# An 8-head graph attention layer: target rows of four of a group's eight tiles gathered by GpSimd instead of spread by TensorE

## The chip, the cores and the metric

One core of a Trainium2 chip (trn2). The time is that of the device, in microseconds (us), for one execution of the whole program, seven graph layers one after the other; with several runs it is their median.

## The reference, cut to what matters

A graph of 3125 nodes with 256 features and 53125 edges (25000 pairs in both directions and a self loop for each node), the edges sorted by their target `dst`. Seven layers of message passing run one after the other: layer 0 is a graph attention layer with 8 heads and edge features, layers 1 to 3 are SAGE convolutions, layer 4 is a GCN, layers 5 and 6 are attention layers with 4 heads. The change touches layer 0 alone:

```python
h = (x @ W.T).reshape(n, H, D)                       # n = 3125, H = 8, D = 32
h_src, h_dst = h[src], h[dst]
alpha = einsum('ehd,hd->eh', h_src, a_src) + einsum('ehd,hd->eh', h_dst, a_dst)
enc = relu(edge_attr @ edge_W.T + edge_b).reshape(-1, H, D)
alpha = leaky_relu(alpha + sum(enc * h_dst, axis=-1), 0.2)
ex = exp(alpha - segment_max(alpha, dst)[dst])
attn = ex / segment_sum(ex, dst)[dst]
out = segment_sum(h_src * attn[..., None], dst) + bias
```

What the change is about is `h_dst`, the row of each edge's target node, which is multiplied by the encoded edge features `enc` and summed per head.

## The kernel before, in words

**Tiles and groups.** The edges are padded to 416 tiles of 128, and 8 tiles make a group, so that there are 52 groups in each layer. Since the edges are sorted by target, the targets of one tile lie within a window of 128 consecutive nodes, and those of a group are added to the accumulator `acc` window by window.

**The table.** Ahead of layer 0 the node rows are written to a table in HBM, `tables[0]`, with 272 floats a row: 8 scores, and for each of 8 heads one score and 32 features (together 264 floats, columns `H` to `TW`).

**Source rows.** POOL (GpSimd) gathers the rows of the source nodes with an indirect DMA for each tile (L1791), 8 a group, into one of four row buffers. From the fifth group on it waits first for `rows_free`, which VectorE gives in `add_group` (L1227) once a group has been added to the accumulator. POOL does this for all seven layers, and in layer 0 nothing else.

**Target rows.** For the target side, SyncE loads for each tile the 128 consecutive table rows of its window into `spans` (L1693, in `edge_tables`), two tiles a quarter, q = 0 to 3, each quarter with a semaphore `span_landed[q]` of its own. Ahead of a quarter's load it waits for `h_ready`, so that the quarter's spans of the group before have been read. VectorE makes one-hot matrices of the edges' targets (L1120), and TensorE spreads the window's rows to the edges with two matmuls a quarter (`spread`, L478; the profile shows each as two instructions). The result stands in PSUM, in `h_ps`, one buffer of two tiles, so a spread waits until VectorE has used the quarter before (`prod_ready`).

**Encoding, product and sum.** TensorE also encodes the edge features (`encode`, L465), ScalarE takes them out of PSUM (`encoded`, L916), VectorE multiplies them by the target rows (`products`, L1128) and sums them per head (`reductions`, L1134).

**The order of a step.** Each engine has the order of a step written out by hand (`step`, in `edge_pe`, `edge_act` and `edge_dve`), for three groups at once: group g is summed up, group n = g + 1 gets its scores and segment maxima, and group m = g + 2 gets its products. TensorE's step is: encode and spread quarter 0 of m, encode 1, the sums of g's first four tiles (L513), the transposed scores of n (L485), spread 1, encode 2, the edges of the scans (L490), spread 2, encode 3, the carries (L497), the sums of g's other four tiles, spread 3, the shifts turned back (L502), the sums turned (L526, L527) and the rescaling (L507). VectorE's step is: messages of g (L1182), the one-hots of g + 3, `add_group` of g - 1 (L1196, L1198), product 0, scores of n, messages, reduction 0, scans (L1149, L1150), product 1, carry (L1156 to L1162), reduction 1, product 2, maxima (L1167 to L1173), reduction 2, rescale, product 3 and reduction 3. ScalarE takes the node sums out of PSUM at L933, as soon as `node_ready` says that L513 is done.

Of the kernel before, what the change touches and what calls it, by code (L numbers as in the profile page):

```python
# [28 lines left out]
ALU = mybir.AluOpType  # L29
# [18 lines left out]
TW = D + 16  # L48
# [20 lines left out]
ATTR = 4 * PAD_E // P  # L69
HEAD = D // 8 + 1  # L70
ASIDE = 16 * (4 + 3 * 4)
SUM_BUFS = 4
# [12 lines left out]
def gnn_program(nc, a, out, stop):  # L85
    last_stage = NL - 1 if stop is None else stop
    ctx = ExitStack()
    with ctx:
# [139 lines left out]
        src_landed = [sem(f"src_landed{b}") for b in range(SUM_BUFS)]  # L228
        span_landed = [sem(f"span_landed{q}") for q in range(4)]
        high_landed = [sem("high_landed0"), sem("high_landed1")]  # L230
# [217 lines left out]
        def edge_pe(pe, l, turns, sum_turns):  # L448
# [19 lines left out]
            def spread(m, j, h, q):  # L468

                par, turn = pair_of(j, h)  # L470
                if q == 0:
                    pe.wait_ge(edge_turned_ready, m + 1)
                pe.wait_ge(span_landed[q], 32 * (m + 1))
                if not (q == 0 and isinstance(m, int) and m == 0):
                    pe.wait_ge(prod_ready, 4 * m + q)
                for i in range(2):
                    k = 2 * q + i
                    ins = mm(ps[:, i, 0:TW], edge_turned[:, par, k, :], spans[:, k, :], start=True, stop=True)  # L478
                ins.then_inc(h_ready, 1)
# [628 lines left out]
        def edge_dve(dve, l, ch, turns, sum_turns):  # L1108
# [14 lines left out]
            def products(m, q):  # L1123

                at = 4 * m + q
                dve.wait_ge(enc_copied, at + 1)
                dve.wait_ge(h_ready, at + 1)
                V.tensor_tensor(prod[:, q % 2, :, :], enc[:, q % 2, :, :], h_ps[:, :, H:TW], ALU.mult).then_inc(prod_ready, 1)  # L1128

# [501 lines left out]
        def _(sp):  # L1631
# [45 lines left out]
            def edge_tables(x, h, par):  # L1677
# [9 lines left out]
                sp.dma_start(attr[:, par, :], attr_parts[:, bass.ds(x * T * P, T * P)]).then_inc(attr_landed[par], 16)  # L1687
                for q in range(4):
                    if not (early and x == 0):
                        sp.wait_ge(h_ready, 4 * x + q - 3)  # L1690
                    for k in (2 * q, 2 * q + 1):
# [39 lines left out]
        def _(pool):  # L1731
# [41 lines left out]
            for l in range(n_edge_layers):  # L1773
# [10 lines left out]
                for g in range(NG):  # L1784
# [5 lines left out]
                    for k in range(T):  # L1790
                        pool.indirect_dma_start(  # L1791
                            src_rows(l, par)[:, k, :], None, tables[l][:, :],
                            bass.IndirectOffsetOnAxis(ap=src_idx[:, g * T + k:g * T + k + 1], axis=0)
                            ).then_inc(src_landed[par], 16)


# [178 lines left out]
```

## Time and profile before

| what | value |
|---|---|
| time, median of 3 runs | 6083.94 us (6080.36 to 6095.35) |
| profiled execution, its own time | 6029.88 us |
| its span, first to last instruction | 6028.1 us |
| granted TensorE clock, mean over the span | 0.721 of full speed |
| busy share of the span, PE, DVE, ACT, POOL | 57%, 35%, 19%, 47% |
| HBM read, written | 512.47 MB, 31.37 MB |

A page of the profile shows one execution. Engines: PE is TensorE's matmuls, PEld its weight loads, DVE is VectorE, ACT ScalarE, POOL GpSimd, SP SyncE. L1791 is line 1791 of the kernel. A row of a group of instructions gives engine, operation, what it writes and reads, count, busy time and mean length of one in ns, then the idle time of its engine just ahead of it and what ended that. "remote" stands where the profile finds no instruction whose end released the wait at that moment. Layer 0 lies between some 83 and 1070 us of the span.

### The profile page before, as it was taken

Reading aid. Unit: us, or ns where it says so; the run is one execution under the profiler, and the core shown is the slowest. Engines: PE = TensorE matmul, PEld = TensorE weight load, DVE = VectorE, ACT = ScalarE, POOL = GpSimd, SP = SyncE. Lnnn points to the kernel's source line nnn. Section 1 sums busy time; section 2 is a strip of 40 time slices with the busy share of each in tenths; the row PEclk is TensorE's granted clock in tenths of the full one; section 3 lists DMA queues with packets and bytes.
Section 4 is the critical chain, followed back from the end, with each engine's and each line's share of the span. In section 5 each row is a group of like instructions: output and inputs, shape, how many; then the busy total and the mean of one; then the engine's idle time right before and its main releaser. Section 6 shows DMA issues by size and latency. Waiting matters only on the chain.

```text
span 6028.1 us, 63366 instructions
## 1 busy us (share of the span) xinstructions
PE 3460.3 (57%) x14514; PEld 2370.1 (39%) x14515; DVE 2116.7 (35%) x5850; ACT 1164.2 (19%) x3033; POOL 2826.4 (47%) x3013
## 2 busy tenths in 40 slices
PE   4777778835446444454446644444665663665665
PEld 2555455524334333333334433333443442443443
DVE  3666666512111111111113211123444444444445
ACT  1333333200001000010000100003332323332232
POOL 2444444066553665646663366643554532444540
PEclk7878888767668766777667777776666776766676
DMA  5555555022222222223222223222333322333330
GB/s 172 146 143 145 140 142 146 19 87 87 79 80 74 86 86 84 86 80 86 84 84 59 67 84 87 86 58 76 91 92 91 93 72 66 90 91 92 93 84 22
DMA packets 278630, 546.82 MB, mean 91 GB/s; under 512 B 72195, under 2 KB 161079, under 8 KB 278111
## 3 DMA queue, kind: packets, MB, share of 16 engines
q0 software_dynamic: 140416, 391.24, 23.4%
q1 hardware_dynamic: 137951, 152.85, 8.6%
q8 instruction: 71, 1.16, 0.1%
q14 instruction: 192, 1.57, 0.1%
HBM read 512.47 MB, written 31.37 MB: 90 GB/s over the span
## 4 chain that ended last, share of the span: by engine, by line
another core or an unknown queue 36%; PE 32%; issue 14%; DVE 10%; SPq 3%; ACT 2%; DVEq 1%; ACTq 1%; DMA 1%; POOL 0%; POOLq 0%
PE ps L606 9%; PE ps L690 7%; PE ps L857 3%; PE ps L513 2%; PE ps L835 2%; DVE rows L1409 2%; PE ps L478 2%; PE ps L805 1%; PE ps L613 1%; ACTq L338 1%; SPq L1692 1%; ACT rows L1026 1%; PE ps L816 1%; SPq L1693 1%
## 5 line engine op out<-in xcount | busy, mean ns | idle before, releaser
L1791 POOL DMA_INDIRECT rows<-table,src_idx x2912 | 2798.4, 961 | 2804.8 <-issue 864.7
L606 PE MATMUL ps<-rows,attr 128*128 128x256 f32 x3328 | 1068.6, 491 | 170.8 <-issue 100.1
L606 PEld LDWEIGHTS ps<-rows,attr 128*128 128x128 f32 x3328 | 825.7, 255 | 381.0 <-issue 208.7
L613 PE MATMUL ps<-ident,rows 128*128 128x128 f32 x416 | 116.7, 373 | 1184.6 <-ACT rows L1026 901.3
L1302 DVE TENSOR_TENSOR acc<-acc,ps 128x256 f32 x208 | 87.7, 422 | 1933.7 <-PE ps L613 1323.3
L613 PEld LDWEIGHTS ps<-ident,rows 128*128 128x128 f32 x416 | 51.0, 172 | 1267.9 <-ACT rows L1026 957.4
L1297 DVE TENSOR_SCALAR attr<-iota,local 128x128 f32<-128x128 f32 x1664 | 356.7, 298 | 219.2 <-issue 156.0
L690 PE MATMUL ps<-rows,attr 128*128 128x260 f32 x832 | 331.0, 551 | 33.7 <-DVE rows L1409 33.7
L690 PE MATMUL ps<-rows,w_roots 128*128 128x260 f32 x832 | 325.1, 544 | 35.5 <-DVE rows L1409 34.9
L478 PE MATMUL ps<-rT,attr 128*128 128x272 f32 x832 | 282.7, 470 | 63.0 <-DVE norm L1128 24.4
L1026 ACT ACTIVATE rows<-ps,mean_of 128x256 f32<-128x256 f32 x156 | 73.8, 473 | 1251.4 <-remote 824.6
L660 PE MATMUL ps<-ident,al 128*32 128x128 f32 x104 | 38.6, 371 | 467.1 <-DVE al L1372 457.6
L513 PE MATMUL ps<-rows,rT 128*128 128x272 f32 x832 | 296.5, 515 | 6.7 <-DVE rows L1182 6.6
L1371 DVE TENSOR_TENSOR al<-ps,rows 128x32 f32<-128x32 f32 x104 | 19.9, 191 | 679.3 <-remote 673.7
L1409 DVE TENSOR_TENSOR rows<-rows,ps 128x1024 f32<-128x1024 f32 x208 | 249.2, 1198 | 2.9 <-ACT rows L989 1.4
L690 PEld LDWEIGHTS ps<-rows,attr 128*128 128x128 f32 x832 | 211.8, 273 | 95.3 <-DVE rows L1409 38.7
L690 PEld LDWEIGHTS ps<-rows,w_roots 128*128 128x128 f32 x832 | 209.3, 270 | 95.7 <-DVE rows L1409 39.8
L513 PEld LDWEIGHTS ps<-rows,rT 128*128 128x128 f32 x832 | 197.2, 249 | 69.6 <-issue 15.6
L478 PEld LDWEIGHTS ps<-rT,attr 128*128 128x128 f32 x832 | 171.7, 224 | 130.7 <-issue 79.4
L1128 DVE TENSOR_TENSOR norm<-rT,ps 128x528 f32<-128x528 f32 x208 | 144.8, 696 | 191.4 <-PE ps L478 91.0
L660 PEld LDWEIGHTS ps<-ident,al 128*32 128x32 f32 x104 | 10.7, 103 | 497.5 <-issue 497.3
L977 ACT ACTIVATE w_roots<-iota,local 128x128 f32<-128x128 f32 x416 | 127.2, 388 | 390.5 <-DVEq L1452 390.5
(230 smaller groups left out, 4341.8 us busy)
## 6 DMA issues: line engine op xcount, KB each, us to landing
rT<-table SPq DMA_DIRECT2D x416, 136.0 KB
rows<-table,src_idx POOLq DMA_INDIRECT x2912
high_rows<-in_tiles SPq DMA_DIRECT2D x156, 256.0 KB
table<-rows SPq DMA_DIRECT2D x24, 512.0 KB, 2.8
table<-rows SPq DMA_DIRECT2D x12, 528.0 KB, 3.0
pens<-pen_rows SPq DMA_DIRECT2D x52, 96.2 KB
pens<-pen_rows SPq DMA_DIRECT2D x104, 48.1 KB
attr_parts<-acc SPq DMA_DIRECT2D x9, 416.0 KB
```

The lines of the kernel that those rows point to most:

```text
L478: ins = mm(ps[:, i, 0:TW], edge_turned[:, par, k, :], spans[:, k, :], start=True, stop=True)
L513: ins = mm(edge_node_ps[par], edge_hot[par][:, k, :], src_rows(l, b)[:, k, 0:TW], start=k == 0, stop=k == T - 1)
L606: ins = mm(node_ps[par % 2], sum_hot[:, par % 2, k, :], src_rows(l, par)[:, k, 0:D], start=k == 0, stop=k == T - 1)
L613: ins = nc.tensor.transpose(sum_ps[par % 2][f], node_sums[:, par % 2, f * P:(f + 1) * P], ident[:, :])
L690: ins = mm(gat_node_ps[par], gat_hot[par][:, k, :], src_rows(l, b)[:, k, 0:D + H], start=k == 0, stop=k == T - 1)
L857: ins = mm(into, x[:, f, k * P:(k + 1) * P], w_table[s + 1][:, f, 0:w], start=f == 0, stop=f == 1)
L977: ins = nc.scalar.activation(gat_hot[par][:, k, :], iota[:, 0:P], ACT.Abs, scale=-1.0, bias=local[:, bass.ds(g * T + k, 1)])
L1026: nc.scalar.activation(node_sums[:, par % 2, :], node_ps[par % 2], ACT.Copy, scale=mean_of[:, bass.ds(g, 1)] if l in MEAN_LAYERS else 1.0) ...
L1128: V.tensor_tensor(prod[:, q % 2, :, :], enc[:, q % 2, :, :], h_ps[:, :, H:TW], ALU.mult).then_inc(prod_ready, 1)
L1297: return V.tensor_scalar(sum_hot[:, par % 2, k, :], iota[:, 0:P] if w is None else iota[:, bass.ds(w * P, P)], local[:, bass.ds(g * T + k, ...
L1409: V.tensor_tensor(x[:, :, 0:D].rearrange("p t (h d) -> p t h d", h=H), x[:, :, 0:D].rearrange("p t (h d) -> p t h d", h=H), gat_ex_ps[b % ...
L1791: pool.indirect_dma_start(src_rows(l, par)[:, k, :], None, tables[l][:, :], bass.IndirectOffsetOnAxis(ap=src_idx[:, g * T + k:g * T + k + ...
```

## The change

In layer 0, the target rows of the quarters q = 2 and 3, tiles 4 to 7 of each group, are gathered by POOL with an indirect DMA for each tile, by `dst_idx`, straight into the `spans` buffer in SBUF: row e of the buffer is then the target row of edge e itself. TensorE's `spread` returns at once for these quarters, SyncE loads spans only for q = 0 and 1, and VectorE's `products` reads q = 2 and 3 from `spans` in place of PSUM. POOL issues these gathers behind the 8 source gathers of the group, and waits ahead of each pair for the product of the same quarter of the group before. The counts of `h_ready` go from four to two a group.

```diff
--- before.py
+++ after.py
@@ -68,6 +68,7 @@
 SEG_LOADS = {0: 48, 5: 64, 6: 64}
 ATTR = 4 * PAD_E // P
 HEAD = D // 8 + 1
+SPREAD = 2
 ASIDE = 16 * (4 + 3 * 4)
 SUM_BUFS = 4
 ROW_BUFS = [SUM_BUFS] * NL
@@ -226,7 +227,8 @@
         consts = sem("consts")
         built = sem("built")
         src_landed = [sem(f"src_landed{b}") for b in range(SUM_BUFS)]
-        span_landed = [sem(f"span_landed{q}") for q in range(4)]
+        span_landed = [sem(f"span_landed{q}") for q in range(SPREAD)]
+        far_landed = [sem(f"far_landed{q}") for q in range(SPREAD, 4)]
         high_landed = [sem("high_landed0"), sem("high_landed1")]
         attr_landed = [sem("attr_landed0"), sem("attr_landed1")]
         edge_turned_ready = sem("edge_turned_ready")
@@ -467,12 +469,14 @@
 
             def spread(m, j, h, q):
 
+                if q >= SPREAD:
+                    return
                 par, turn = pair_of(j, h)
                 if q == 0:
                     pe.wait_ge(edge_turned_ready, m + 1)
                 pe.wait_ge(span_landed[q], 32 * (m + 1))
                 if not (q == 0 and isinstance(m, int) and m == 0):
-                    pe.wait_ge(prod_ready, 4 * m + q)
+                    pe.wait_ge(prod_ready, 4 * m + q if q > 0 else 4 * m + SPREAD - 4)
                 for i in range(2):
                     k = 2 * q + i
                     ins = mm(ps[:, i, 0:TW], edge_turned[:, par, k, :], spans[:, k, :], start=True, stop=True)
@@ -1124,8 +1128,13 @@
 
                 at = 4 * m + q
                 dve.wait_ge(enc_copied, at + 1)
-                dve.wait_ge(h_ready, at + 1)
-                V.tensor_tensor(prod[:, q % 2, :, :], enc[:, q % 2, :, :], h_ps[:, :, H:TW], ALU.mult).then_inc(prod_ready, 1)
+                if q < SPREAD:
+                    dve.wait_ge(h_ready, SPREAD * m + q + 1)
+                    far = h_ps
+                else:
+                    dve.wait_ge(far_landed[q - SPREAD], 32 * (m + 1))
+                    far = spans[:, 2 * q:2 * q + 2, :]
+                V.tensor_tensor(prod[:, q % 2, :, :], enc[:, q % 2, :, :], far[:, :, H:TW], ALU.mult).then_inc(prod_ready, 1)
 
             def reductions(m, q):
                 if q == 0 and not (isinstance(m, int) and m == 0):
@@ -1685,9 +1694,9 @@
                 if not early:
                     sp.wait_ge(enc_ready, 4 * x - 4)
                 sp.dma_start(attr[:, par, :], attr_parts[:, bass.ds(x * T * P, T * P)]).then_inc(attr_landed[par], 16)
-                for q in range(4):
+                for q in range(SPREAD):
                     if not (early and x == 0):
-                        sp.wait_ge(h_ready, 4 * x + q - 3)
+                        sp.wait_ge(h_ready, SPREAD * (x - 1) + q + 1)
                     for k in (2 * q, 2 * q + 1):
                         node = sp.value_load(tile_base[0:1, bass.ds(x * T + k, 1)], min_val=0, max_val=NPAD - P)
                         sp.dma_start(spans[:, k, :], tables[0][bass.ds(node, P), :]).then_inc(span_landed[q], 16)
@@ -1792,6 +1801,15 @@
                             src_rows(l, par)[:, k, :], None, tables[l][:, :],
                             bass.IndirectOffsetOnAxis(ap=src_idx[:, g * T + k:g * T + k + 1], axis=0)
                             ).then_inc(src_landed[par], 16)
+                    if kind == "gat_edge":
+                        for q in range(SPREAD, 4):
+                            if g > 0:
+                                wait_alone(pool, prod_ready, 4 * (g - 1) + q + 1)
+                            for k in (2 * q, 2 * q + 1):
+                                pool.indirect_dma_start(
+                                    spans[:, k, :], None, tables[l][:, :],
+                                    bass.IndirectOffsetOnAxis(ap=dst_idx[:, g * T + k:g * T + k + 1], axis=0)
+                                    ).then_inc(far_landed[q - SPREAD], 16)
 
 
         @block.tensor
```

## Rows read from the trace of the kernel before

**Rows 1.** The page: span, part 1 (busy time), part 5 (the gathers).
```profile
span 6028.1 us, 63366 instructions
...
PE 3460.3 (57%) x14514; PEld 2370.1 (39%) x14515; DVE 2116.7 (35%) x5850; ACT 1164.2 (19%) x3033; POOL 2826.4 (47%) x3013
...
L1791 POOL DMA_INDIRECT rows<-table,src_idx x2912 | 2798.4, 961 | 2804.8 <-issue 864.7
```

**Rows 2.** Groups of instructions by line, 159.5 to 1052 us (layer 0's steady part).
```profile
L1791 POOL DMA_INDIRECT rows<-table,src_idx x384 | 389.9, 1015 | 523.3 <-DVEq L1227 414.6 <-issue 108.7
...
L478 PE MATMUL ps<-rT,attr 128*128 128x272 f32 x768 | 255.5, 462 | 38.2 <-DVE norm L1128 23.5 <-issue 11.7 <-DMA rT<-table 2.8
```

**Rows 3.** Timeline of POOL: first and last batch begun in layer 0's steady part.
```profile
159.59 0.94 POOL L1791 DMA_INDIRECT rows<-table,src_idx  x1 [32.65 <-DVEq L1227]
...
1030.34 0.94 POOL L1791 DMA_INDIRECT rows<-table,src_idx  x1 [4.91 <-DVEq L1227]
```

**Rows 4.** Timeline of one short step, 870 to 886 us (start, length, engine, line).
```profile
870.42 0.94 POOL L1791 DMA_INDIRECT rows<-table,src_idx  x1 [5.12 <-DVEq L1227]
...
871.43 1.22 DVE L1182 TENSOR_TENSOR rows<-rows 128x1024 f32<-128x1024 f32 x1
871.67 1.79 POOL L1791 DMA_INDIRECT rows<-table,src_idx  x1 [0.30 <-issue]
...
876.36 2.10 PE L513 MATMUL ps<-rows,rT 128*128 128x272 f32 x8
...
880.07 0.95 POOL L1791 DMA_INDIRECT rows<-table,src_idx  x1 [0.30 <-issue]
...
882.35 0.39 ACT L933 ACTIVATE rT<-ps 128x256 f32<-128x256 f32 x1 [4.94 <-remote]
882.48 0.70 DVE L1128 TENSOR_TENSOR norm<-rT,ps 128x528 f32<-128x528 f32 x1 [3.07 <-remote]
...
886.35 0.94 POOL L1791 DMA_INDIRECT rows<-table,src_idx  x1 [5.33 <-DVEq L1227]
```

**Rows 5.** Busy time in stretches of that step: engines, TensorE's clock, DMA share, GB/s.
```profile
875.40:879.60 4.20, 4.17 (x21) 2.74 (x19) 3.45 (x11) 1.97 (x4) 3.29 (x4) 1.00 0.81 198
879.60:882.30 2.70, 0.00 (x0) 0.00 (x0) 0.00 (x0) 0.00 (x0) 1.12 (x2) 1.00 0.60 177
```

**Rows 6.** Timeline of two longer steps, 511 to 552 us.
```profile
516.86 0.39 PE L497 MATMUL ps<-one,carry_th 1*64 1x1 f32 x4
...
520.85 0.95 POOL L1791 DMA_INDIRECT rows<-table,src_idx  x1 [0.31 <-issue]
...
523.55 0.73 DVE L1170 SCALAR_TENSOR_TENSOR segmax<-pens,ps,segmax 64x128 f32<-64x128 f32 x2 [4.80 <-remote]
...
529.34 0.94 POOL L1791 DMA_INDIRECT rows<-table,src_idx  x1 [7.55 <-DVEq L1227]
...
551.53 0.94 POOL L1791 DMA_INDIRECT rows<-table,src_idx  x1 [12.34 <-DVEq L1227]
```

**Rows 7.** Waits, 159.5 to 1049.5 us: total, times, longest.
```profile
ACT rT L933 <- remote: 111.2, 24, 5.9
...
DVE norm L1128 <- remote: 71.7, 25, 6.1
```

**Rows 8.** Busy time in stretches of the layer's start, and of its steady part.
```profile
106.00:129.00 23.00, 3.08 (x7) 1.43 (x7) 3.17 (x6) 1.19 (x2) 16.07 (x17) 0.50 0.47 127
129.00:152.00 23.00, 18.62 (x61) 10.87 (x62) 14.17 (x32) 5.97 (x17) 0.00 (x0) 0.60 0.40 103
159.50:1049.50 890.00, 700.37 (x2729) 449.95 (x2727) 580.86 (x1340) 327.11 (x910) 389.91 (x384) 0.81 0.53 144
```

**Rows 9.** Timeline at the start of the layer.
```profile
86.67 1.11 POOL L1791 DMA_INDIRECT rows<-table,src_idx  x1 [78.91 <-DMA table<-rows]
...
125.99 0.95 POOL L1791 DMA_INDIRECT rows<-table,src_idx  x1 [0.30 <-issue]
...
129.00 0.41 DVE L1149 TENSOR_TENSOR_SCAN fwd<-pens,ps 64x128 f32<-64x128 f32 x1 [7.26 <-remote]
```

## The prediction, made before the change was run

> **What bounds the kernel now.** I read the page first, then the groups by line of layer 0 (the 8-head layer), then POOL's timeline in it, and last the stretches between POOL's batches of gathers. The page [rows 1] shows no engine near full over the whole run, and POOL with 2912 gathers as its only real work. Layer 0's steady part has 384 of them, 48 batches of 8, and POOL waits once ahead of each batch, 414.6 us in all, for rows_free from VectorE [rows 2]. So POOL is not the bound: it runs at the pace of the steps. First batch to last is 870.75 us over 47 steps [rows 3], **18.5 us a step**.
>
> The steps are of two kinds. The short one of rows 4 takes 15.9 us; its like (16.6 us and less from batch to batch) comes 17 times in 47, with a mean of 15.9. The other 30 have a mean of (870.75 - 17 x 15.9) / 30 = 20.0; rows 6 show one.
>
> What the reader is to see in both is a dead stretch late in POOL's batch. In the short step, TensorE's last sums before it run from 876.36 to 878.46. ScalarE waits for them (node_ready) and gets going only at 882.35, 3.9 us later; VectorE's last product waits as long [rows 4]. From 879.6 to 882.3 TensorE, VectorE and ScalarE all do nothing; only POOL and the DMAs work [rows 5]. In the longer step TensorE's carries end at 517.25 and VectorE, which needs them, starts at 523.55 [rows 6]. Both releases come just behind the batch: the last gather ends at 881.02 and 521.80, the work starts 1.3 and 1.75 us later. The waits that the profile can only call "remote" are these, 111.2 us on one line of ScalarE and 71.7 us on one of VectorE [rows 7]. **My reading: signals between engines arrive late while a batch of gathers is running, from some 4 us after its start, and arrive together once its last data has landed.** The layer's start says it loudest. POOL gathers without a break there, from 86.67 to 126.94 [rows 9]. From 106 to 129 TensorE is busy for 3.1 of 23 us and VectorE for 3.2; in the next 23 us, with no gathers, 18.6 and 14.2 [rows 8]. A scan that waited since 121.7 starts at 129.0 [rows 9].
>
> **The change, part by part.**
> *Removed on TensorE:* the spreads of tiles 4 to 7, 8 of a group's 16 instructions of L478. 255.5 us / 768 = 0.33 us each [rows 2], 2.7 us a group. In the short step they lie ahead of the dead stretch, where TensorE has the time; only in longer steps is part of it behind the release. I credit 0.5 us to a longer step and nothing to a short one; the ends are 0 and 2.7.
> *Removed on SyncE:* 4 of 8 span loads with their register loads, and the waits on h_ready for them. TensorE's L478 waits for those loads only 2.8 us in all [rows 2], so: 0. The bytes are the same ones, on the other queue.
> *Added on POOL:* 4 gathers a group. A plain one takes 0.95 us and 0.30 of issue before it [rows 4], 1.25 in all; over the first run it is (125.99 - 86.67) / 31 = 1.27 [rows 9]. 12 are 15.0 us where 8 were 10.0. POOL would be busy 15.0 of 18.5 us, so it does not become the bound by count, but its batch is longer, and with it the dead stretch. The pair for tiles 4 and 5 waits for product 2 of the group before, which is mostly done by then: it follows the eight at once, +2.5 us. The pair for tiles 6 and 7 waits for product 3. What is queued behind that wait is only the next group's eight, which need rows_free, later still in VectorE's order; and the rows land a whole step before their product, so lateness of the data costs 0.
> *Short step:* products 2 and 3 no longer need h_ready, so product 3 is not held as it is at 882.48 [rows 4]; all 12 gathers run on, +5.0. VectorE then has that product behind it at the release, -0.7. Step: 15.9 + 5.0 - 0.7 = 20.2, **+4.3**.
> *Longer step:* the release moves by the one pair, +2.5; TensorE's share, -0.5. The last pair runs behind the release and may hold signals there or bring the next batch's hold forward; bounds 0 and 2.5, and I take 0.5, since the first 4 us of a run of gathers hold little and this run is 2.5 us. Sum **+2.5**.
> *48 steps:* (17 x 4.3 + 30 x 2.5) / 47 = 3.15 each, 151 us.
> *The layer's start:* 16 more gathers in the first run, 16 x 1.25 = 20 us; this is the dead run of rows 8. **+20.** (Below: 0, if the waits inside split the run.)
> *VectorE's product from SBUF:* L1128 now reads two operands in SBUF for half of its instructions. No row has that shape; the nearest is L1182, two SBUF operands, 1024 elements in 1.22 us, against 0.70 us for 528 [rows 4], the same time per element: 0 for VectorE. But beside that L1182 (871.43 to 872.65) a gather takes 1.79 us in place of 0.95. Two such products of 0.70 us a group can each stretch a gather by up to 0.8; I take 0.3 a step, **+14**; bounds 0 and 80.
> The page "SBUF — State Buffer" of the Trainium skill, section "Who interferes with whom", says that a VectorE instruction with two SBUF inputs contends with a GpSimd one that reads SBUF. By that rule, this change makes such instructions of 104 products. By the row the same follows with a price; the rule agrees.
> Sum: 151 + 20 + 14 = 185. The profiled execution took 6029.88 us (span 6028.1), 54 below the median of 6083.94 (6080.36 to 6095.35). The layer's extra time does not depend on which one it is added to: 6084 + 185 = **6269, say 6270**.
>
> **Rivals.**
> *A, faster: the hold does not grow with the batch.* The place is the release after a batch. If a late signal is late by a fixed 4 to 5 us each, however many gathers follow, four more cost nothing and TensorE's 2.7 us come off. For it: the two delays above are 3.9 and 6.3 us, not wildly apart, and TensorE is busy 700 of 890 us [rows 8]. Against it: both end right behind the batch. The step is then 18.5 - 2.5 = 16.0, just above POOL's own 15.0 and its wait: -2.5 x 48 = -120, 5965. It decides from where the release stays at 11.5 to 12 us after the batch's start. 0.10.
> *B, within 0.3%.* Both effects exist and cancel, or the longer batch falls where TensorE had work anyway. 0.05.
> *C, much slower: gathers nearly merge into one run.* If the last pair's hold meets the next batch, each step is like the layer's start: 15.0 us of gathers with little done in them, plus 1.5, plus all that now runs in the open. Priced by the second step of rows 6, from 529.34 to 551.53, 22.2 us: with the pair 24.7, against 18.5, is 6.2 x 48 = 298, with the start 318, 6400; upward of that to 6500. For it: rows 8. Against it: the pair is short. 0.16.
> *D, the loads return less than thought but the sign holds* (+20 to +90, the hold grows for the longer steps only): 0.05.
> That the change does not do what it says: the spreads and loads of tiles 4 to 7 are gone from the code in every group, so it has no chance of its own.
>
> **How the numbers follow.** The forecast, +90 to +300, has 0.64. Its own range is 6175 to 6385. For 8 in 10 I take 6130 to 6430: it leaves out A, B and the far end of C. 0.3% is 18 us, about what can be told from no change here. Faster 0.10, same 0.05, slower 0.85 (the forecast, C and D).
>
> **What would show it.** L478 with 416 instructions in place of 832, L1791 with 208 more, other layers unchanged. POOL's batches in layer 0 at 12 gathers in a row or 10 and 2, and the release 1.3 to 1.8 us behind the tenth or twelfth. Steps near 20.2 where they were 15.9, and 22.5 where they were 20.0; "remote" waits of ScalarE and VectorE longer in total; TensorE's granted clock in the layer below the 0.81 of rows 8, as its idle stretches are longer. The forecast is wrong if the steps shorten, if the release comes ahead of the batch's end, or if the time is lost at POOL itself (waits for rows_free near zero), or outside layer 0.

## The result, and the profile after

The kernel after takes **6192.99 us** (median of 4 runs, 6181.10 to 6200.22) against 6089.65 us for the kernel before beside it (4 runs, 6080.36 to 6106.73): ratio 1.017, 95% interval 1.0151 to 1.019. That is **slower by 103 us** where the prediction had 186 more than before, 6270 us, with a range of 6130 to 6430. The profiled execution took 6193.65 us.

From the page of the kernel after: the span, part 1 and the two lines of gathers in part 5 [rows 1].

```profile
span 6191.9 us, 61252 instructions
...
PE 3399.5 (55%) x14098; PEld 2320.0 (37%) x14099; DVE 2121.6 (34%) x5850; ACT 1159.2 (19%) x3033; POOL 3055.6 (49%) x3221
...
L1800 POOL DMA_INDIRECT rows<-table,src_idx x2912 | 2813.4, 966 | 2522.4 <-issue 892.7
...
L1809 POOL DMA_INDIRECT rT<-table,dst_idx x208 | 214.0, 1029 | 210.1 <-DVE norm L1137 154.0
```

POOL has 208 more gathers, 229 us more work. TensorE has 416 instructions fewer and 61 us less work. VectorE's work is the same. So the edit did what it says; its effect on time has to be looked for in the waits.

Where the time went: from the first gather of layer 0 to the first of layer 1 are 1124.9 us before and 1223.7 after, **98.8 more in the layer that was changed**. (The two profiled executions are 164 us apart, since the one of before was 60 below its median; the rest of that is spread over layers whose code is the same.) In layer 0 the first of POOL's waits for `rows_free` now comes at 162.92 and the last batch at 1131.13, 47 steps of **20.60 us** where there were 18.53 [rows 3].

Groups by line of the kernel after, from 162.9 to 1131.1 us [rows 2]:

```profile
L1800 POOL DMA_INDIRECT rows<-table,src_idx x376 | 388.1, 1032 | 196.7 <-issue 121.9 <-DVEq L1236 74.3 <-DVE norm L1137 0.6
...
L1809 POOL DMA_INDIRECT rT<-table,dst_idx x188 | 193.8, 1031 | 190.1 <-DVE norm L1137 139.2 <-issue 50.9
```

L1236 is `add_group`, L1137 the products. POOL waited 414.6 us for `add_group` before; now 74.3 for it and 139.2 for products. It has work or issue for 388.1 + 193.8 + 121.9 + 50.9 = 755 of 968 us, 16.1 of a step's 20.6: nearer to the bound than the 15.0 of 18.5 I forecast. Before, POOL waited for `add_group` ahead of every batch; in 26 of the 47 steps after, it does not wait there at all, and the next batch follows its own queue. But no other engine waits for a row that POOL gathers: among all waits of these 968 us none is for a DMA.

Stretches of the kernel after [rows 8]; columns: start and end, length, busy time and count of PE, PEld, DVE, ACT, POOL, granted TensorE clock, DMA share, GB/s:

```profile
106.00:129.00 23.00, 6.25 (x17) 2.90 (x17) 3.67 (x8) 0.60 (x1) 15.78 (x17) 0.50 0.46 134
129.00:152.00 23.00, 11.17 (x40) 6.79 (x40) 11.37 (x24) 7.16 (x18) 12.43 (x12) 0.65 0.44 128
162.90:1131.10 968.20, 637.75 (x2306) 397.75 (x2305) 577.80 (x1316) 316.35 (x894) 581.92 (x564) 0.72 0.45 130
```

The clock went from 0.81 to 0.72 in the steady part, with TensorE busy 66% of it and not 79%. The same matmul is longer at it: one of L478 took 462 ns on average before [rows 2] and takes 517 after (L482). The layer's start did not grow by 20 us: the waits for products split the run, and the fifth group's batch comes at 162.92 where it came at 159.59, **+3.3**.

Waits of the kernel after, 162.9 to 1131 us (total, times, longest) [rows 7]:

```profile
POOL rT L1809 <- DVE norm L1137: 139.2, 42, 6.6
ACT rT L920 <- remote: 135.1, 33, 11.0
...
ACT rT L937 <- remote: 117.9, 20, 10.9
```

L937 is the old L933, 111.2 us and 5.9 at the longest before, L920 the old L916. The longest "remote" wait of ScalarE has gone from 7.9 us (L916) to 11.0. I call it a hold when engines stand in such waits while a run of gathers is on or has just ended.

One step of the kernel after, in its timeline (start, length, engine, line):

```profile
183.56 0.94 POOL L1800 DMA_INDIRECT rows<-table,src_idx  x1 [0.74 <-issue]
...
192.20 0.60 ACT L920 ACTIVATE rT<-ps 128x512 f32<-128x512 f32 x1 [4.67 <-remote]
192.42 0.95 POOL L1800 DMA_INDIRECT rows<-table,src_idx  x1 [0.30 <-issue]
...
195.07 0.29 DVE L1165 TENSOR_TENSOR_SCAN carry_row<-edge_pen_row,ps 1x72 f32<-1x72 f32 x1 [3.52 <-remote]
...
196.52 0.69 DVE L1137 TENSOR_TENSOR norm<-rT 128x528 f32<-128x528 f32 x1
...
198.02 0.98 POOL L1809 DMA_INDIRECT rT<-table,dst_idx  x1 [4.64 <-DVE norm L1137]
...
199.42 0.69 DVE L1137 TENSOR_TENSOR norm<-rT 128x528 f32<-128x528 f32 x1
...
200.92 0.95 POOL L1809 DMA_INDIRECT rT<-table,dst_idx  x1 [0.67 <-issue]
...
203.46 0.40 DVE L1207 TENSOR_TENSOR acc<-acc,ps 128x256 f32 x1
204.25 0.95 POOL L1800 DMA_INDIRECT rows<-table,src_idx  x1 [0.75 <-DVEq L1236]
```

The eight gathers run to 193.37; ScalarE and VectorE get going at 192.20 and 195.07 after 4.67 and 3.52 us of "remote". **Product 2 of the group before, at 196.52, is itself behind the hold**, so the pair for tiles 4 and 5 does not follow the eight at once, as I had it: it comes at 198.02, when the release is long past. The last gather is issued at some 202.2 and the next batch follows at 204.25: the 12 gathers lie as 8, 2 and 2 over the whole step. In 19 of the 47 steps the first pair came only behind the release like this, after a wait of 4.5 us and more; in 5 it waited 0.3 to 2.5 us, and in 23 it followed the eight at once.

Only one step of 47 is still 16.6 us or less, where 17 were. Another kind of step, in which all 12 gathers go in a row and the next eight follow without a pause (POOL's and VectorE's lines; the last three lie in the step behind it):

```profile
287.22 0.95 POOL L1800 DMA_INDIRECT rows<-table,src_idx  x1 [0.89 <-DVEq L1236]
...
292.85 0.69 DVE L1137 TENSOR_TENSOR norm<-rT 128x528 f32<-128x528 f32 x1
293.13 1.43 POOL L1800 DMA_INDIRECT rows<-table,src_idx  x1 [0.30 <-issue]
...
295.86 0.71 DVE L1137 TENSOR_TENSOR norm<-rT 128x528 f32<-128x528 f32 x1
296.12 1.27 POOL L1800 DMA_INDIRECT rows<-table,src_idx  x1 [0.30 <-issue]
...
299.38 0.40 DVE L1207 TENSOR_TENSOR acc<-acc,ps 128x256 f32 x1
...
303.38 0.95 POOL L1809 DMA_INDIRECT rT<-table,dst_idx  x1 [0.30 <-issue]
304.63 0.95 POOL L1800 DMA_INDIRECT rows<-table,src_idx  x1 [0.30 <-issue]
...
305.54 0.70 DVE L1137 TENSOR_TENSOR norm<-rT,ps 128x528 f32<-128x528 f32 x1 [5.75 <-remote]
...
313.91 0.95 POOL L1800 DMA_INDIRECT rows<-table,src_idx  x1 [0.30 <-issue]
...
316.99 0.41 DVE L1158 TENSOR_TENSOR_SCAN fwd<-pens,ps 64x128 f32<-64x128 f32 x1 [8.60 <-remote]
```

`add_group` is done at 299.78, but the next batch starts at 304.63, when POOL has got through its queue: 17.4 us from batch to batch, where about 13 would have been enough for `add_group`. What this costs is again a hold, and not a wait for rows. The 20 gathers from 287.22 to 314.86 are one run; VectorE's next product 0 comes at 305.54 after 5.75 us of "remote", its scan at 316.99, 2.1 us behind the run's end, after 8.60. Seven such runs of 14 to 24 gathers lie in these 47 steps; before there was none longer than 8. The two gathers that begin beside a product with both operands in SBUF take 1.43 and 1.27 us, not 0.95.

### The profile page after: what moved, and what is told of

Read it like the earlier page. It is cut to its first block, busy times and chain, and to the rows that moved or that the text cites. A ratio compares the mean times of both kernels' runs of the same rounds, so it can differ in the third digit from the quotient of the medians.

```text
span 6191.9 us, 61252 instructions
## 1 busy us (share of the span) xinstructions
PE 3399.5 (55%) x14098; PEld 2320.0 (37%) x14099; DVE 2121.6 (34%) x5850; ACT 1159.2 (19%) x3033; POOL 3055.6 (49%) x3221
## 4 chain that ended last, share of the span: by engine, by line
another core or an unknown queue 42%; PE 28%; issue 13%; DVE 9%; ACT 4%; DVEq 1%; DMA 1%; ACTq 1%; SPq 0%; POOL 0%; POOLq 0%
PE ps L610 7%; PE ps L694 6%; PE ps L861 3%; DVE rows L1418 2%; PE ps L517 2%; PE ps L839 2%; PE ps L482 1%; PE ps L809 1%; ACT rT L907 1%; PE ps L617 1%; PE ps L467 1%; PE ps L820 1%; ACT rows L1030 1%; DVE attr L1373 1%
## 5 line engine op out<-in xcount | busy, mean ns | idle before, releaser
L517 PE MATMUL ps<-rows,rT 128*128 128x272 f32 x832 | 330.1, 562 | 1.6 <-DVE rows L1191 1.6
L1809 POOL DMA_INDIRECT rT<-table,dst_idx x208 | 214.0, 1029 | 210.1 <-DVE norm L1137 154.0
L1380 DVE TENSOR_TENSOR al<-ps,rows 128x32 f32<-128x32 f32 x104 | 19.9, 192 | 689.0 <-remote 683.4
L517 PEld LDWEIGHTS ps<-rows,rT 128*128 128x128 f32 x832 | 218.5, 276 | 75.7 <-issue 19.9
L981 ACT ACTIVATE attr<-iota,local 128x128 f32<-128x128 f32 x416 | 127.2, 388 | 380.2 <-DVEq L1461 380.2
L920 ACT ACTIVATE rT<-ps 128x512 f32<-128x512 f32 x208 | 123.6, 594 | 376.6 <-remote 170.2
```

What stands on the lines that cost most here:

```text
L517: ins = mm(edge_node_ps[par], edge_hot[par][:, k, :], src_rows(l, b)[:, k, 0:TW], start=k == 0, stop=k == T - 1)
L981: ins = nc.scalar.activation(gat_hot[par][:, k, :], iota[:, 0:P], ACT.Abs, scale=-1.0, bias=local[:, bass.ds(g * T + k, 1)])
L1809: pool.indirect_dma_start(spans[:, k, :], None, tables[l][:, :], bass.IndirectOffsetOnAxis(ap=dst_idx[:, g * T + k:g * T + k + 1], axis=0) ...
```

## The experiments

The kernels of one session ran on one chip beside the kernel before, and each is compared with that alone. This matters here, for the kernel before took 6101.84 and 6112.84 us in the first and fourth session, and **4773.27 and 4770.33 us in the second and third**, all its runs of a session within 0.7%. Its code and the length of one gather (0.95 us) are the same in both. I call them the *late* and the *clean* condition, for what the traces show: late has the "remote" waits of the text above, clean has none at all in layer 0's steady part. Sessions 3 and 4 were on the same chip, so the chip does not decide it. The result above, and the trace that the prediction was made from, are of the late one.

The table gives all runs. The times of a step and of the layer are those of one profiled execution each, the ratios those of all runs, and the two need not agree: the profiled execution of the kernel before took 6029.88 us, 72 and 83 less than its medians in sessions 1 and 4, and that of e4 was the slowest of its ten, 32 us above their median, that of e2 the fastest of its five, 27 below. "Layer 0" is from its first gather to that of layer 1 in the profiled execution, "step" the mean of POOL's 47 steps from the fifth group on, "remote" the sum of such waits, of all engines, over these steps.

| run | session, condition | ratio to before (95%) | layer 0, us | step, us | remote, us |
|---|---|---|---|---|---|
| before | the trace of the prediction, late | 1 | 1124.9 | 18.53 | 365.6 |
| after | late | 1.017 (1.0151 to 1.019) | 1223.7 | 20.60 | 483.0 |
| e1_no_gathers | 1, late | 0.9877 (0.9843 to 0.9911) | 1059.8 | 17.36 | 221.7 |
| e2_extra_gathers | 1, late | 1.0251 (1.0219 to 1.0282) | 1271.9 | 21.55 | 590.9 |
| e3_extra_narrow | 1, late | 1.0216 (1.0185 to 1.0247) | 1285.5 | 21.78 | 652.9 |
| e4_spread3 | 1, late | 1.0051 (1.0034 to 1.0067) | 1193.5 | 20.01 | 414.0 |
| e5_paced_late | 2, clean | 0.9995 (0.9986 to 1.0005) | 873.4 | 13.86 | 0 |
| e6_paced_early | 2, clean | 0.9994 (0.9984 to 1.0003) | 875.5 | 13.86 | 0 |
| e7_paced_after | 2, clean | 1.0256 (1.0239 to 1.0273) | 998.9 | 16.29 | 0 |
| e8_extra_16rows | 2, clean | 1.0192 (1.0171 to 1.0212) | 968.2 | 15.88 | 0 |
| a1_change_again | 3, clean | 1.0267 (1.0247 to 1.0286) | 1001.3 | 16.40 | 0 |
| a2_paced_again | 3, clean | 1.0001 (0.9991 to 1.0011) | 875.6 | 13.80 | 0 |
| a3_spread3_again | 3, clean | 0.9977 (0.9967 to 0.9987) | 868.8 | 13.83 | 0 |
| a4_no_gathers_again | 4, late | 0.9885 (0.9844 to 0.9927) | 1047.0 | 17.06 | 181.4 |

The last column keeps the order of the steps in the late condition: 181 and 222 us of "remote" with the removed work gone, 366 before, 414, 483 and 591 to 653 with two and four more gathers a step. In the clean one it is 0 for every kernel, with 8, 10 or 12 gathers.

Where the "remote" waits end can be counted against POOL's gathers. Before, 88 of 106 (317.5 of 365.6 us) end within 2.5 us behind the last gather of a run and the other 18 while one is on; in e2 it is 100 of 126 (490 of 591 us). After the change it is only 53 of 120 (251 of 483 us), and 62 (201 us) end while gathers are running. So the trace before and e2 bear out the prediction's reading that the waits are let go behind the batch, while with the runs of up to 24 gathers many are let go earlier.

### e1_no_gathers: the change without its gathers

The spreads and loads of tiles 4 to 7 are gone and nothing takes their place, so the edge term of the scores is left out for half of the tiles (`spans` holds zeros there).

```diff
             ch = ...
+            ch.then(V.memset(spans[:, 4:8, :], 0.0))
...
-                    dve.wait_ge(far_landed[q - SPREAD], 32 * (m + 1))
...
-                    if kind == "gat_edge":
-                        for q in range(SPREAD, 4):
...
```

> The change without its gathers: no spreads and no loads for tiles 4 to 7, no gathers in their place; VectorE multiplies by a buffer of zeros that is never refreshed, so the scores of half of the tiles leave out the edge term. Theory H (gathers hold the signals of other engines; what TensorE saves lies mostly in held time): step of layer 0 between 17.2 and 18.2 us against 18.5 before, the whole 15 to 65 us faster than before. Theory T (TensorE is the bound of a step, the 2.7 us of spreads come off in full): step 15.8 to 16.2, 110 to 130 us faster.

Measured: 6028.79 us, -75 by the ratio, more than the 15 to 65 expected and less than TensorE's 2.7 us in full. This is what the removed work gives back: I had credited 0.5 us to 30 of the steps, 15 us. The step's mean falls by 1.2 us (18.53 to 17.36). The run takes out the span loads together with the spreads, so it does not show how much is TensorE's. POOL's gathers are untouched there (376 from 154.4 to 970.2 us), and the clock does not rise (0.77).

What I had not looked at is VectorE's wait for the spreads. In the trace before (159.5 to 1049.5 us) its products waited for them by

```profile
DVE norm L1128 <- PE ps L478: 77.6, 53, 3.5
```

and of this, over the 47 steps, 67 us (1.4 a step) lay ahead of the products of quarters 2 and 3, whose spreads the change takes away, and 35 us of "remote" ahead of product 2. In e1 these are gone, but 52 us of waiting for the spread of quarter 0 have come up, where there were none.

### e2_extra_gathers: the gathers without the change

The kernel before, and behind each group's eight gathers four more by `dst_idx` into a buffer that nothing reads.

```diff
+                    if kind == "gat_edge":
+                        for q in range(2, 4):
+                            if g > 0:
+                                wait_alone(pool, prod_ready, 4 * (g - 1) + q + 1)
+                                wait_alone(pool, extra_landed[q - 2], 32 * g)
+                            for k in (2 * q, 2 * q + 1):
+                                pool.indirect_dma_start(
+                                    spare[:, k - 4, :], None, tables[l][:, :], ...
+                                    ).then_inc(extra_landed[q - 2], 16)
```

> The kernel before, with the change's four gathers a group added at the same place of POOL's queue and behind the same waits, into a buffer that nobody reads. Theory H: the gathers are the whole cost: step 20.6 to 21.6, 100 to 150 us slower than before, at least as slow as the change. Rival P (the cost is in VectorE's product with two SBUF operands, or in products that wait for far rows): gathers alone cost under 40 us.

Measured: 6256.09 us, **+153**. Nothing reads these rows and no other work was added, so the four gathers alone cost more than the whole change (100 to 150 were expected). POOL itself does not set this pace: it waits 245.9 us for products ahead of the added gathers. Waits from 160 to 1000 us, the added gathers in the groups by line, and the stretch of the layer's steady part:

```profile
DVE norm L1130 <- remote: 153.6, 32, 7.8
...
ACT rT L935 <- remote: 125.9, 16, 10.0
```

```profile
L1803 POOL DMA_INDIRECT spare<-table,dst_idx x188 | 214.1, 1139 | 290.0 <-DVE norm L1130 245.9 <-issue 43.8 <-DVEq L1229 0.3
```

```profile
162.00:1174.90 1012.90, 732.61 (x2688) 467.99 (x2688) 573.26 (x1320) 324.57 (x898) 591.10 (x564) 0.75 0.54 151
```

VectorE's products, held for 71.7 us in all before [rows 7], are held for 153.6 in these 840 us, and ScalarE for 10.0 us at the longest. The granted clock is 0.75, not 0.81, and the same matmuls take 733 us and not 684. Whether part of the 153 us comes by way of these slower matmuls was not separated.

### e3_extra_narrow: the same gathers with 64 bytes a row

```diff
-                                    spare[:, k - 4, :], None, tables[l][:, :],
+                                    spare[:, k - 4, 0:16], None, tables[l].rearrange("n (w o) -> (n w) o", o=16),
```

> As the one with extra gathers, but each of the added gathers fetches 64 bytes a row in place of 1088. The count of descriptors and POOL's work stay, the bytes go down to a seventeenth. If the hold comes from POOL's issuing and the descriptors: within 25 us of the wide extra gathers. If it comes from the bytes on the way: less than half of their cost. POOL's own time for one gather should stay at 0.95 us in both.

Measured: 6241.30 us, +132, with 17 times fewer bytes in the added gathers. The intervals of e2 and e3 overlap. (With the same indices on a table seen as rows of 16 floats, the added gathers also read other addresses.) The lines of its waits and of the instructions that write `spare` (least, median, longest ns):

```profile
ACT rT L935 <- remote: 158.4, 20, 10.2
...
DVE norm L1130 <- remote: 131.7, 28, 7.8
```

```profile
L1803 POOL DMA_INDIRECT spare<-table,dst_idx x208: 942/947/1790, 98.1 to 1211.0; - x104
```

So the bytes are not the main cause; what is left is the number of gathers, or of their 128 rows, or the time that POOL spends on them, and these are the same for both widths.

### e4_spread3 and a3_spread3_again: half of the change

```diff
-SPREAD = 2
+SPREAD = 3
```

Only tiles 6 and 7 are gathered, ten gathers a step.

> The change for tiles 6 and 7 only: TensorE spreads three quarters, POOL gathers one pair a group, behind product 3 of the group before. Theory H with a cost in proportion to the gathers: about half of the change, 40 to 65 us slower than before, step 19.4 to 19.8. If the cost comes from the pair that waits for product 2 and pushes everything behind it: under 25 us. If even a single pair merges with the next batch: as slow as the change, 90 us or more.

> The change for tiles 6 and 7 only, 10 gathers a group. It cost 31 us on a chip with late signals (1.0051). On a chip without them, theory Q: 10 x 1.25 to 1.36 is 12.5 to 13.6 us, just under a step, so within 25 us of before, with a gain of up to 25 for TensorE's two spreads less; if the gathers cost in proportion there too, 50 to 65 us slower.

Measured: 1.0051 in the late condition (+31 us, less than half of the change and less than the 40 to 65 expected), **0.9977 in the clean one, -11 us**. Both intervals leave out 1, though both effects are small: the sign depends on the condition.

### e5_paced_late, e6_paced_early, a2_paced_again: fewer gathers in a row

The kernel before with waits that spread POOL's batch over the step (e6 has `k // 2` without the 1; a2 is e5).

```diff
                     for k in range(T):
+                        if kind == "gat_edge" and g >= ROW_BUFS[l] and k in (2, 4, 6):
+                            wait_alone(pool, prod_ready, 4 * (g - 1) + k // 2 + 1)
```

> The kernel before, its eight source gathers of a group given out in pairs: the first behind rows_free as before, the others behind products 1, 2 and 3 of the step, from the fifth group on in layer 0. Nothing is added or removed. Theory H (a hold sets in after some 4 us of gathers in a row and lasts to their end): pairs of 2.5 us with gaps hold little, step 16.5 to 17.8 against 18.5, 35 to 95 us faster. Rival W (what counts is the gather work, not how it is cut, or the last pair runs into the next batch): between 20 us faster and 60 us slower.

> As the late pacing, each pair one product earlier: behind products 0, 1 and 2. In a short step the pairs then follow with almost no gap, and only a step that is held up is cut. Theory H: between 0 and 50 us faster than before. Rival W: within 20 us of before.

> The late pacing of the source gathers again (nothing added, pairs behind products 1, 2 and 3). On a chip without late signals it was no different (0.9995). On one with late signals, H in its form of a hold after 4 us of gathers in a row: 35 to 95 us faster; W: between 20 us faster and 60 us slower.

Measured: 0.9995, 0.9994 and 1.0001, no difference. These three were to test the hold, but ran where there was none to remove. All they tell is that in the clean condition none of these pacings gains or loses anything. **Pacing in the late condition was not tried**, so whether a hold needs several gathers in a row stays open. What they did give is a trace of the clean condition with nearly the kernel before in it. Its longest waits (a2, 136 to 785 us), its gathers in the groups by line, and its stretch:

```profile
ACT rT L916 <- PE ps L465: 158.6, 125, 3.7
...
ACT rT L933 <- PE ps L513: 81.4, 47, 3.4
...
DVE norm L1128 <- PE ps L478: 43.2, 66, 2.3
```

```profile
L1793 POOL DMA_INDIRECT rows<-table,src_idx x376 | 429.3, 1142 | 227.2 <-issue 105.2 <-DVE norm L1128 95.8 <-DVEq L1227 26.2
```

```profile
136.40:785.20 648.80, 583.56 (x2675) 382.04 (x2673) 565.34 (x1316) 319.12 (x892) 429.28 (x376) 0.94 0.69 193
```

The same ScalarE line that was held 24 times, up to 5.9 us, by "remote" [rows 7] now waits for TensorE's sums themselves, 47 times in 47 steps and 3.4 us at most. A step takes 13.8 us, not 18.5. TensorE's granted clock is 0.94 there, not 0.81, and the same 2675 matmuls take 584 us, not 684: the two conditions differ in the clock too, and no run separates it from the missing holds. Layer 0 makes 249 of some 1260 us between the two profiled executions; the rest lies in the other layers.

### e8_extra_16rows: the extra gathers with 16 rows each

```diff
-                                    spare[:, k - 4, :], ... dst_idx[:, ...]
+                                    spare[0:16, k - 4, :], ... dst_idx[0:16, ...]
```

> The kernel with the extra gathers, each of the added ones for 16 rows in place of 128: the same count of gather instructions and waits, an eighth of their descriptors. If the cost is with the descriptors: 0 to 50 us slower than before (the full ones cost 150). If it is with the instruction itself, whatever its rows: 120 us slower or more. POOL's own time for one shows how much of its 0.95 us goes by rows.

Measured: 1.0192, +92 us, in the clean condition. That is neither of the two ranges expected, which were laid against the 153 us of the late one; the full-width extra gathers were not run in the clean one. Its gathers' lines:

```profile
L1803 POOL DMA_INDIRECT spare<-table,dst_idx x208: 832/852/1940, 97.2 to 909.0; - x104
```

```profile
L1793 POOL DMA_INDIRECT rows<-table,src_idx x376 | 381.3, 1014 | 114.6 <-issue 108.8 <-DMA spare<-table,dst_idx 4.0 <-DVE norm L1130 1.8
...
L1803 POOL DMA_INDIRECT spare<-table,dst_idx x188 | 193.2, 1027 | 57.3 <-issue 55.2 <-DMA spare<-table,dst_idx 1.5 <-DVE norm L1130 0.6
```

With an eighth of the rows a gather still takes POOL 0.85 us in the median. Work and issue are 381.3 + 193.2 + 108.8 + 55.2 = 738.5 of 746.6 us: **POOL has no time left**, and steps take 15.9.

### e7_paced_after and a1_change_again: the change in the clean condition

e7 is the kernel after with e6's waits, a1 the kernel after as it is.

> The changed kernel with its source gathers in pairs behind products 0, 1 and 2, its far pairs behind products 2 and 3 as they are. Theory H: 0 to 60 us faster than the change, still slower than before, for there are more gathers than gaps: 40 to 100 us slower than before. Rival W: as the change, 90 to 120 us slower than before.

> The changed kernel unaltered, beside the one before, on whatever chip it gets. The earlier runs fell on two kinds of chip: one where the kernel before takes 6080 to 6120 us and signals come late while gathers run, one where it takes 4770 us and they do not. Theory H (late signals make the cost): 90 to 120 us slower on a chip of the first kind, under 40 on one of the second. Theory Q (on a chip without late signals POOL's queue is the bound, 12 gathers of 1.25 us and more against a step of 13.9): there 16.0 to 16.6 us a step, 105 to 135 us slower, POOL without a pause between its batches.

Measured: 1.0256 and 1.0267, +122 and **+128 us**. Pacing changes nothing again. The gathers of a1 in the groups by line, its longest wait of VectorE, its timeline at 508 us and its stretch:

```profile
L1800 POOL DMA_INDIRECT rows<-table,src_idx x377 | 419.6, 1113 | 114.9 <-issue 109.1 <-DVE norm L1137 5.2 <-DVEq L1236 0.6
...
L1809 POOL DMA_INDIRECT rT<-table,dst_idx x188 | 180.5, 960 | 57.3 <-issue 57.3
```

```profile
DVE norm L1137 <- DMA rT<-table,dst_idx: 111.3, 48, 4.4
```

```profile
508.39 0.95 POOL L1809 DMA_INDIRECT rT<-table,dst_idx  x1 [0.30 <-issue]
508.72 0.71 DVE L1137 TENSOR_TENSOR norm<-rT 128x528 f32<-128x528 f32 x1 [4.28 <-DMA rT<-table,dst_idx]
509.64 0.95 POOL L1800 DMA_INDIRECT rows<-table,src_idx  x1 [0.30 <-DVE norm L1137]
```

```profile
148.10:919.00 770.90, 596.01 (x2303) 374.05 (x2302) 575.25 (x1318) 323.42 (x894) 599.08 (x565) 0.79 0.58 163
```

POOL waits for anything but its own issue for 5.8 of 771 us. Once a step VectorE waits for target rows that are still being gathered (4.28 us at 508.72), and no "remote" plays a part. 12 gathers of 1.06 us (600.1 / 565, stretched ones included) and 0.30 of issue are 16.3 us, and a step is 16.40. Ten of them are 13.6 by the same sum. The rows of a3, 139.8 to 789.6 us, have the same:

```profile
L1800 POOL DMA_INDIRECT rows<-table,src_idx x377 | 401.0, 1064 | 116.7 <-issue 110.0 <-DVE norm L1137 4.0 <-DVEq L1236 2.8
L1809 POOL DMA_INDIRECT rT<-table,dst_idx x94 | 102.9, 1094 | 30.4 <-issue 27.7 <-DVE norm L1137 2.1 <-DVEq L1236 0.6
```

Work and issue are 641.6 of 649.8 us. POOL is full there too, but at 13.83 us a step, which is what the step took anyway (13.80 in a2), so nothing is lost. The granted clock of a1 is 0.79 and not the 0.94 of a2; since POOL has no gap left, the slower matmuls are not what sets its step. Where its gain of 11 us comes from is not in the mean step; layer 0 as a whole is 6.8 us shorter than in a2.

### a4_no_gathers_again: e1 in the late condition once more

> The change without its gathers again (spreads and loads of tiles 4 to 7 gone, VectorE multiplies by a buffer of zeros instead, so half of the tiles leave out the edge term). It was 75 us faster on a chip with late signals (0.9877). On a chip without them, theory Q: TensorE's side is worth 1 to 2 us a step, 50 to 100 us faster than before, and the whole 180 to 230 us between this kernel and the change is POOL's queue. If VectorE or ScalarE is the bound of a step there: under 30 us faster.

Measured: 0.9885 (0.9844 to 0.9927), 6027.87 us against 6112.84. e1's 75 us are confirmed (70 by this ratio), and the step is 17.06. What the removed work is worth in the clean condition was therefore not measured.

## Why the prediction was right or wrong

**The bound: right for the condition it was read in.** POOL was not the bound there, and the engines were held in "remote" waits that grow with the gathers. e2 shows it: four gathers that nobody needs cost 153 us and add 225 us of such waits, and their bytes hardly matter (e3). Where these waits are absent, nearly the kernel before (a2) needs 13.8 us a step in place of 18.5, at a higher clock. What the hold is at bottom stays open. It is not a matter of gathers alone, since equal gathers run in the clean condition without it.

**The mean step, +3.15 forecast, 151 us.** Measured +2.07, and 97 us over 47 steps. Two terms were off, and both made the forecast too high. The gathers were priced too dear: without the credits the forecast has 5.0 for a short step and 3.0 for a longer one, (17 x 5.0 + 30 x 3.0) / 47 = 3.7, and with the start and the stretched gathers 213 us; e2 has +3.02 a step and +153 us in all. The removed work was priced too cheap, and this is the step of the argument that failed: "I credit 0.5 us to a longer step and nothing to a short one", 15 us, or 27 with the 0.7 of the short steps' product; e1 measures 75. "In the short step they lie ahead of the dead stretch, where TensorE has the time" took a stretch without a wait of TensorE to be a stretch with slack, while VectorE waited 67 us for just these spreads. With that work gone the "remote" waits themselves fell from 366 to 222 us. Which of the two the 75 us come from, and what share is owed to the loads, is not shown. The two errors make 60 + 48 = 108 us too much; the forecast is off by only 83, since the change costs 25 more than its two halves measured alone. That those 25 came to its help is luck.

**"It follows the eight at once, +2.5": wrong in 19 of 47 steps.** The pair for tiles 4 and 5 waits for product 2, and that product was behind the hold. These steps have a mean of 21.6 us and the other 28 one of 19.9, so a late pair did not make its step a cheap one. What the place of the pair costs or saves by itself is not shown.

**"It does not become the bound by count": right in the late condition, wrong in the clean one.** The count was right for the mean, 15.0 of 18.5. In the late condition POOL's queue does set when the next batch starts (26 of 47 steps), and so joins batches into longer runs, but no engine waits for its rows. In the clean condition it is the whole of the loss: POOL has no gap, and VectorE waits for rows once a step. I priced the gathers at 1.25; with those stretched beside two-SBUF instructions they are 1.36 there.

**The layer's start, +20: wrong, +3.3.** My lower bound of 0 had the reason: the waits for products split the run. I chose the other end.

**Two-SBUF products, +14: the effect is there, and of the size forecast in POOL's time.** A product itself takes as long from SBUF as from PSUM (696 and 701 ns). In the trace after, of 93 gathers that run beside a product from PSUM (and beside no L1191) none takes over 1.1 us, and their mean is 0.95; of 67 beside a product with both operands in SBUF 29 do, and their mean is 1.14. That is 67 x 0.19 = 13 us of POOL's time in the steady part. The mean of all gathers does not show it (1015 ns before [rows 2], 1032 after, and 1048 in e2, which has no such product), since it goes by how many lie beside L1182 too. The page "SBUF — State Buffer" of the Trainium skill, section "Who interferes with whom", says that a VectorE instruction with two inputs in SBUF contends with a GpSimd instruction that reads SBUF. It also infers that `tensor_tensor` does not hold up the generation of DMA descriptors, since that needs the write side of the shared ports. The stretched gathers agree with the first sentence and not with this inference. What POOL's 13 us cost the kernel in the late condition is not shown. The gathers alone are +153 and the removed work -75, which would make +78; the change is +103. The 25 us between can be these stretched gathers or the way the two effects meet in a step; VectorE's new wait for target rows is not the cause, since it does not occur in the trace after.

**The signs I named.** L478 (now L482) has 416 instructions, L1809 has 208, other layers keep theirs, "remote" waits are longer, and the clock in the layer fell from 0.81 to 0.72. The steps I expected at 20.2 and 22.5 have a mean of 20.6 in place of 21.7. One sign against the forecast did appear in part: "if the release comes ahead of the batch's end". Half of the "remote" waits after the change, 62 of 120, end while a run of gathers is on.

**The rivals.** A, that the hold is fixed and the sign turns: wrong, by e2. C, that gathers merge into one run: wrong in sum, but it happens, in the seven runs of 14 to 24 gathers; the wait of 11.0 us at L920 ends 2.2 us behind one of them. That the same change costs 103 us in the condition with holds and 128 us by POOL's queue in the other was no rival of mine.

## What to carry to other kernels

When work moves to a queue, lay the queue's length against the step of every condition in which the kernel runs: POOL's 16.3 us were under the 18.5 of one condition and over the 13.8 of the other, and only there did the queue set the time. When work is taken from an engine, look for who waits for its results before its place is called slack. For indirect gathers count instructions, not bytes or rows, and set 1.25 us for each (0.95 and 0.30 of issue in these traces), more beside VectorE instructions with both operands in SBUF. Before believing a cost that comes from waits with no releaser in the profile, run the kernel before again in another session: here the same code took 22% less time, and half of the change was a small gain there and a small loss here.

## What the runs showed of the hardware that was not expected

- **Two conditions, 6100 and 4770 us, for one kernel.** All runs within a session agree, sessions 3 and 4 on one chip do not. In the late one, engines wait up to 7.9 us (before) and 11.0 us (after) for nothing that the profile can name, while gathers are running; TensorE's granted clock in layer 0 is 0.81 in one and 0.94 in the other (before, a2). What sets the condition was not found.
- **A gather's time on POOL depends little on its size**: median 852 ns for 16 rows, 947 ns for 128 rows of 64 bytes, and 0.95 us for 128 rows of 1088 bytes, each with 0.30 of issue.
- **A gather is slowed by VectorE's two-SBUF instructions, and not by the same product read from PSUM**: beside products from SBUF 29 of 67 gathers took over 1.1 us, beside products from PSUM none of 93 (the trace after).
- **In the late condition gathers that nobody reads slow the other engines**: four more a step are +153 us and 225 us more of "remote" waits (e2), hardly less with 64 bytes a row (e3).
